# Involution on one core: the running maximum of the logits taken chunk by chunk out of PSUM instead of tap row by tap row out of SBUF

## What is computed

```python
sub2 = x1[:, :, None] - unfold_patches(x2)            # 49 taps, 32 channels
feat = jnp.concatenate([sub2, subp], axis=1)
y = relu(bn_eval(feat, bn1_g, bn1_b, bn1_m, bn1_v))
y = relu(bn_eval(conv1x1(y, cw1), bn2_g, ...))
wgt = softmax(conv1x1(y, cw2, cb2), axis=2)           # over the 49 taps
for i in range(7):
    for j in range(7):
        out = out + patch(x3, i, j) * wgt[:, :, 7 * i + j][:, :, None]
```

## Time and profile before

| | |
|---|---|
| median of 3 runs | 3697.45 us |
| span of the profiled execution, first to last instruction | 3768.7 us |
| step 1 of the third slot, and of the last (15th) | 352.09 and 1635.56 us of the span |
| busy share over the span: PE, DVE, ACT, POOL | 81%, 68%, 53%, 54% |
| mean granted TensorE clock | 0.919 of full speed |

### The profile page before, as it was taken

One profiled execution on the slowest core, in us unless ns is written; L12 is line 12 of the kernel. 1 busy time (PEld: TensorE's weight loads), 2 busy tenths in 40 slices (PEclk: granted clock), 3 DMA queues, 4 the chain that ended last, 5 costly groups with the idle time before them and its releaser, 6 DMA issues. The chain is left out here.

```text
span 3768.7 us, 102003 instructions
## 1 busy us (share of the span) xinstructions
PE 3044.6 (81%) x42638; PEld 1539.3 (41%) x42638; DVE 2563.3 (68%) x2229; ACT 2010.5 (53%) x3451; POOL 2040.6 (54%) x1112
## 2 busy tenths in 40 slices
PE   4767788877777788764999899989999987586797
PEld 1224444433443444432433434343435343364565
DVE  6359999999999999996745755574667456443212
ACT  1175566666555566632676666657566754333120
POOL 1169888889898888874622434060416123332422
PEclk9889999999899999896999999999999998797898
DMA  5621111211111112103111111210221112343344
GB/s 195 194 76 47 58 37 58 61 58 59 52 56 50 57 35 61 51 12 97 27 27 64 41 27 37 74 29 19 61 69 28 27 45 98 115 132 113 123 134 127
DMA packets 169418, 257.31 MB, mean 68 GB/s; under 512 B 81584, under 2 KB 128600, under 8 KB 165912
## 3 DMA queue, kind: packets, MB, share of 16 engines
q1 hardware_dynamic: 157120, 219.82, 19.2%
q0 software_dynamic: 11360, 30.95, 2.6%
q10 hardware_dynamic: 504, 0.05, 0.0%
HBM read 152.23 MB, written 79.27 MB: 61 GB/s over the span
## 5 line engine op out<-in xcount | busy, mean ns | idle before, releaser
L741 PE MATMUL ps<-prod,ident 32*32 32x504 f32 x17472 | 936.4, 646 | 259.4 <-issue 182.7
L678 DVE TENSOR_TENSOR prod<-ps,win 128x3584 f32<-128x3584 f32 x280 | 1054.6, 3789 | 97.6 <-PE ps L741 50.9
L1405 POOL TENSOR_TENSOR pool<-kv 128x768 f32<-128x768 f32 (+1 forms) x200 | 349.8, 1756 | 541.5 <-ACT kv L1539 494.4
L741 PEld LDWEIGHTS ps<-prod,ident 32*32 32x32 f32 x17472 | 382.7, 108 | 464.1 <-issue 412.5
L1583 ACT ACTIVATE phq<-ps 128x896 f32<-128x896 f32 x448 | 391.3, 919 | 80.4 <-PE ps L1915 76.8
L456 POOL TENSOR_TENSOR y<-a1w,x2w 128x1568 f32<-128x1568 f32 x98 | 346.0, 3538 | 132.0 <-PE ps L722 114.9
L465 POOL TENSOR_TENSOR ex<-lg,mx 128x1568 f32<-128x1568 f32 x98 | 345.1, 3541 | 16.1 <-DVE mx L664 15.9
L1915 PE MATMUL ps<-qst,sel 96*128 96x448 bf16 x1120 | 297.2, 362 | 17.0 <-ACT sx L1568 8.4
L560 ACT ACTIVATE ps<-ex 128x448 f32<-128x448 f32 x280 | 148.4, 533 | 296.6 <-DVE prod L678 296.6
L1690 DVE TENSOR_TENSOR pool<-ps,kv 128x1280 f32<-128x1280 f32 (+1 forms) x200 | 295.4, 1480 | 1.1 <-ACT ps L1543 1.1
L482 POOL TENSOR_TENSOR own_a<-ex,win 128x1792 f32<-128x1792 f32 x70 | 262.2, 3746 | 45.9 <-issue 21.6
(11 more groups left out here) (266 smaller groups left out, 5306.3 us busy)
## 6 DMA issues: line engine op xcount, KB each, us to landing
win<-planes SPq DMA_DIRECT2D x14, 2480.0 KB, 9.0
pf<-pf_dram SPq DMA_DIRECT2D x392, 55.1 KB
qst<-qsp SPq DMA_DIRECT2D x96, 196.0 KB, 4.8
planes<-stage SPq DMA_DIRECT2D x7, 1984.0 KB, 7.0
xs<-in_x SPq DMA_DIRECT2D x8, 1568.0 KB, 22.0
conv_dram<-osb SPq DMA_DIRECT2D x56, 224.0 KB, 4.9
t<-in_x SPq DMA_DIRECT2D x28, 448.0 KB, 4.0
xt<-conv_dram SPq DMA_DIRECT2D x28, 448.0 KB, 7.6
```

The source lines that it names most:

```text
L678: v.tensor_tensor(o, w, xw, ALU.mult).then_inc(prod_ready, 1)
L741: mm = pe.matmul(ps[32 * h:32 * h + 32, 4 + r, 0:DENC], diag(ident, r), x[32 * r:32 * r + 32, h].rearrange("p s w -> p (s w)"), start=begi ...
L1405: pool.tensor_tensor(phk[j % 2][0:r, :, ROT_V * DH:FLIN].rearrange("p h (r i) -> p h r i", i=DH), ki.unsqueeze(2).broadcast_to([r, HPG, RO ...
```

## The change

The maximum is now taken from the chunks while they lie in PSUM. `chunkmax(c)` replaces `rowmax`: for chunks 2 to 13, in step c + 3, DVE does two instructions of 128x392, one for each bank, that add the bias and take the maximum with what is there so far. DVE takes bank 1 first while ACT copies bank 0 (`third(c, 0)`), then they change places: ACT's `third(c, 1)` waits for DVE's bank 1, and DVE's bank 0 waits for `third(c, 0)`. The copy of a chunk is thus two instructions, and they come one step later on ACT, with `weights` between them. PE's first(c + 1) waits for both readers. `fold` has four passes instead of three, writes its first pass to banks 0 and 1, and comes in step 16 instead of 17. On PE the order within a step changes from first, pair half 0, second, pair half 1 to pair half 0, first, pair half 1, second. Two more waits are added (PE's first chunk on `maxed`, POOL's last shift on `logit`).

```diff
-MAX_AT = [CH_AT[2 * i + 1] + 3 for i in range(K7)]
+MAX_AT = [t + 2 for t in CH_AT]
 FOLD_AT = MAX_AT[-1]
-EXP_NOW = {FOLD_AT + 1: 0, FOLD_AT + 2: 1}
+EXP_NOW = {18: 0, 19: 1}
...
+                if i == K7 - 1:
+                    pool.wait_ge(logit, 2 * b.g(NCH))
...
-                def third(c):
-                    act.wait_ge(mm2, a.g(c) + 1)
+                def third(c, q):
+                    i, h, k = c // 2, c % 2 * 2 + q, chain_bank(b, c) + q
+                    if q == 0:
+                        act.wait_ge(mm2, a.g(c) + 1)
+                        if b and c % 2 == 0:
+                            act.wait_ge(shifted, b.q(i) + 1)
+                    elif c >= 2:
+                        act.wait_ge(ranmax, NMAX * a.n + 2 * c - 3)
+                    act.activation(lg[:, i, h].rearrange("p j w -> p (j w)"), ps[:, k, 0:CW],
                                    ACT.Identity, bias=par[:, CB2:CB2 + 1]).then_inc(logit, 1)
...
                 for u in range(NPAIR_D if b else 0):
-                    if a and u in CH_AT:
-                        second(CH_AT.index(u))
+                    if a and u - 1 in CH_AT:
+                        third(CH_AT.index(u - 1), 0)
                     if b and u + 2 < NPAIR_D:
                         weights(b, u + 2)
+                    if a and u - 1 in CH_AT:
+                        third(CH_AT.index(u - 1), 1)
                     if b and u + 1 < NPAIR_D:
                         denominators(b, u + 1)
                     if a and u in CH_AT:
-                        third(CH_AT.index(u))
+                        second(CH_AT.index(u))
...
-                    v.tensor_tensor(run[:], lg[:, i], lg[:, 0] if i == 1 else run[:], ALU.max).then_inc(ranmax, 1)
+                    for q in (1, 0):
+                        h, k = c % 2 * 2 + q, chain_bank(b, c) + q
+                        if q == 1:
+                            v.wait_ge(mm2, a.g(c) + 1)
...
+                        else:
+                            v.wait_ge(logit, 2 * a.g(c) + 1)
+                        so_far = (lg[:, 0, h] if c < 4 else run[:, h]).rearrange("p j w -> p (j w)")
+                        v.scalar_tensor_tensor(run[:, h].rearrange("p j w -> p (j w)"), ps[:, k, 0:CW], par[:, CB2:CB2 + 1], so_far,
+                                               ALU.add, ALU.max).then_inc(ranmax, 1)
...
+                    v.wait_ge(logit, 2 * a.g(NCH))
+                    v.tensor_tensor(three, rows[:, :, :, 0:3 * W], rows[:, :, :, 4 * W:], ALU.max).then_inc(ranmax, 1)
...
+                    v.tensor_tensor(left, three[:, :, :, 0:W], rows[:, :, :, 3 * W:4 * W], ALU.max).then_inc(ranmax, 1)
...
+                        if c >= 3:
+                            pe.wait_ge(ranmax, NMAX * a.n + 2 * c - 4)
+                        await_ge(logit, 2 * a.g(c))
...
                 for u in range(NPAIR_D if b else 0):
-                    if a and u in CH_AT:
-                        first(CH_AT.index(u))
                     if b:
                         pair(u, 0)
                     if a and u in CH_AT:
+                        first(CH_AT.index(u))
+                    if b and 2 * u + 1 < ND:
+                        pair(u, 1)
+                    if a and u in CH_AT:
                         second(CH_AT.index(u))
```

More of the change, by code:

```diff
@@ L339 @@
 SCALE_AT = 1
-NMAX = K7 + 1
+NMAX = 2 * (NCH - 2) + 3
 class Blk:
@@ L598, in slot @@
                         if c >= 1:
-                            third(c - 1)
+                            third(c - 1, 0)
+                            third(c - 1, 1)
                         if c % 2 == 0 and c + 2 < NCH:
                             first(c // 2 + 1)
-                    third(NCH - 1)
+                    third(NCH - 1, 0)
+                    third(NCH - 1, 1)
                     expo(a, 0)
@@ L645, in slot, with chunkmax @@
             def slot(a, b):
-                def rowmax(i):
-                    if i == 0:
+                def chunkmax(c):
+                    if c < 2:
                         return
[L649 to L653, removed]
-                    v.tensor_tensor(run[:], lg[:, i], lg[:, 0] if i == 1 else run[:], ALU.max).then_inc(ranmax, 1)
@@ L656, in fold @@
-                def fold():
[L657 to L661, removed]
+                    for q in (1, 0):
+                        h, k = c % 2 * 2 + q, chain_bank(b, c) + q
+                        if q == 1:
+                            v.wait_ge(mm2, a.g(c) + 1)
+                            if c < 4:
+                                v.wait_ge(logit, 2 * a.g(c - 2) + 2)
+                            else:
+                                v.wait_ge(ranmax, NMAX * a.n + 2 * c - 6)
+                            if c == 2 and b and not b.early(1):
+                                v.wait_ge(divided, 2 * b.n)
+                        else:
+                            v.wait_ge(logit, 2 * a.g(c) + 1)
+                        so_far = (lg[:, 0, h] if c < 4 else run[:, h]).rearrange("p j w -> p (j w)")
+                        v.scalar_tensor_tensor(run[:, h].rearrange("p j w -> p (j w)"), ps[:, k, 0:CW], par[:, CB2:CB2 + 1], so_far,
+                                               ALU.add, ALU.max).then_inc(ranmax, 1)
@@ new lines, in fold @@
+                def fold():
+                    three = ps[:, 0:2, 0:RW // 2 * 3 * W].rearrange("p b (h x) -> p b h x", x=3 * W)
+                    rows = run[:].rearrange("p (b h) j w -> p b h (j w)", b=2)
+                    left = rows[:, :, :, 0:W]
+                    v.wait_ge(ranmax, NMAX * a.n + 2 * NCH - 4)
+                    v.wait_ge(logit, 2 * a.g(NCH))
+                    v.tensor_tensor(three, rows[:, :, :, 0:3 * W], rows[:, :, :, 4 * W:], ALU.max).then_inc(ranmax, 1)
+                    v.wait_ge(ranmax, NMAX * a.n + 2 * NCH - 3)
+                    v.tensor_tensor(left, three[:, :, :, 0:W], rows[:, :, :, 3 * W:4 * W], ALU.max).then_inc(ranmax, 1)
+                    v.wait_ge(ranmax, NMAX * a.n + 2 * NCH - 2)
+                    v.tensor_tensor(left, three[:, :, :, W:2 * W], left, ALU.max).then_inc(ranmax, 1)
+                    v.wait_ge(ranmax, NMAX * a.n + 2 * NCH - 1)
@@ L662, in fold @@
                     if b:
                         v.wait_ge(shifted, K7 * a.n)
-                    v.tensor_tensor(mx[:].rearrange("p (h w) -> p h w", w=W), run[:, :, 0], run[:, :, 1], ALU.max).then_inc(maxed, 1)
+                    v.tensor_tensor(mx[:].rearrange("p (b h w) -> p b h w", b=2, w=W), three[:, :, :, 2 * W:], left, ALU.max).then_inc(maxed, 1)
                 def pair(p):
@@ L681, in slot @@
                     if a and u in MAX_AT:
-                        rowmax(MAX_AT.index(u))
+                        chunkmax(MAX_AT.index(u))
                     if a and u == FOLD_AT:
@@ L707, in first @@
                     k = chain_bank(b, c)
+                    if c == 0 and not a.early(1):
+                        pe.wait_ge(maxed, a.n)
                     if b is None:
+                        if c >= 4:
+                            pe.wait_ge(ranmax, NMAX * a.n + 2 * c - 6)
                         if c >= 2:
-                            await_ge(logit, a.g(c) - 1)
+                            await_ge(logit, 2 * a.g(c) - 2)
                     else:
-                        await_ge(logit, a.g(c))
+                        if c >= 3:
+                            pe.wait_ge(ranmax, NMAX * a.n + 2 * c - 4)
+                        await_ge(logit, 2 * a.g(c))
                     y, f = y1[a.qpar(i)], pf[a.qpar(i)]
@@ L773, in slot @@
                     if a and u in CH_AT:
+                        first(CH_AT.index(u))
+                    if b and 2 * u + 1 < ND:
+                        pair(u, 1)
+                    if a and u in CH_AT:
                         second(CH_AT.index(u))
                     if b:
-                        if 2 * u + 1 < ND:
-                            pair(u, 1)
                         for k in range(OWN):
```

## The result

| | median | runs |
|---|---|---|
| before | 3695.51 us | 4, 3691.70 to 3697.88 |
| changed | 3775.33 us | 4, 3774.20 to 3777.57 |

The ratio is 1.0216, with an interval of 1.0203 to 1.0228: the changed kernel is 79.8 us slower. 3760 was forecast, with 3694 to 3785 as its range.

The account below looks back on a forecast made before the run. The slot's end was taken as the bound: own 8's start plus a 13.30 us tail, not DVE's work. +5.2 us a slot times 13 is 68, times 0.98 is 66; with 3697.5 about 3762, said 3760, range 3694 to 3785.

Parts of the forecast that it names:

- tail: Slot's end, from the start of POOL's own 8 to the next pair 0: 13.30 us, whatever DVE does.
- fold ready: Slot's end: after both half copies of the last chunk the fold stands ready 84.2 us after pair 0's start.
- The first chunk: Slot's start: PE's first(0) stands behind half of pair 1, so the chunk chain starts 1.0 us later (0 to 1.3).
- The pace: Chunk chain on ACT: 5.13 us a chunk in eleven early steps, 66.5 us for 13 against 65.55, so +1.0 us.
- its relief buys nothing here: Chunk chain: DVE needs 4.85 us a step, less than the chain, so its saved work brings no time there.
- The clash: Slot's end: own 6 starts 0.5 us ahead of the fold, whose first pass waits for it until 87.4.
- The order: Slot's end: pair 16 and PE's own 6 stand behind the fold, delaying own 8; 3.2 of +5.2 us a slot.
- PE's restart: PE after some 6 us idle: pair 16 with own 6 takes 4.8 us, between 3.5 and 5.9.
- The factor 0.98: Scaling of the sum, the profiled execution being 1.9% longer than the median: 68 us becomes 66.
- the fold did meet POOL: Rival at the slot's end: the fold doesn't meet POOL; 3704 with a fast PE, 3723 with a slow one; chance 0.22.
- the half copies were not at half price: Rival on ACT: half copies cost half a whole one, chain at 4.88; with an unblocked fold 3668; chance 0.13.
- the worst case: Rival on DVE: its small instructions clash with POOL too, 3 us each; two a slot give 3840; chance 0.03.

Follow-up runs that it names:

- e1: Changed kernel with the fold moved back to step 17, behind pair 16: 3757.04 us, 10.5 us faster than the kernel before.
- e2: Changed kernel with PE's first chunk of a slot put ahead of pair 1 again: 3837.86 us, 70.3 us slower than the kernel before on that occasion.
- e3: Changed kernel with PE's adding of own 6 moved from the end of step 16 to its beginning: 3757.17 us, 10.4 us faster than the kernel before.
- e4: Changed kernel with ACT copying the maximum's upper columns to PSUM, so the fold's first pass has one SBUF input: 3815.99 us, 48.5 us slower than before.
- e9: Kernel before, whole row maxima kept, with only its last maximum and the fold moved from step 17 to 16: 3774.04 us, 79.4 us slower than before.
- e8: e1 with ACT's weights issued behind both half copies instead of between them: 3652.70 us, 41.9 us faster than the kernel before.
- e7: e8 plus the edits of e2 and e4: 3640.47 us, 54.1 us faster than the kernel before.

## Why the prediction was right, and where its sizes were off

Start of own 8 and start of the next pair 0, from the slot's start, in the slot shown of each kernel. The difference is the tail, the same within 0.4 us.

| | own 8 | next pair 0 | tail |
|---|---|---|---|
| before | 93.22 | 106.52 | 13.30 |
| changed | 99.46 | 112.54 | 13.08 |
| e1 | 92.93 | 106.06 | 13.13 |
| e2 | 99.15 | 112.24 | 13.09 |
| e3 | 92.44 | 105.58 | 13.14 |
| e4 | 96.76 | 110.22 | 13.46 |
| e9 | 97.75 | 110.82 | 13.07 |
| e8 | 90.75 | 103.88 | 13.13 |
| e7 | 88.81 | 101.93 | 13.12 |

That is the step of the prediction that carried the rest: DVE's busy share of 9 was not the bound, own 8's start was. Its other steps, in us from the slot's start:

| step | forecast | measured |
|---|---|---|
| 1. ReLU 0 | 13.9 | 14.82 |
| 2. pace of the early steps | 5.13 | 5.07 |
| ReLU 13 | 80.4 | 80.72 |
| 3. fold ready | 84.2 | 84.41 |
| own 6 starts on POOL | 83.7 | 83.94 |
| fold ends | 89.6 | 89.7 |
| pair 16 and own 6 on PE | 4.8 | 5.63 |
| own 8 starts | 98.4 | 99.46 |
| tail | 13.3 | 13.08 |
| slot | 111.7 | 112.54 |

- **The first chunk** came 1.9 us later than before, not 1.0. I charged PE half a pair at the rate of a busy PE. At that place its clock is at half, and a pair takes it 4.02 us there (the rows in e2). e2 shows that only half of this reaches the slot's end.
- **The pace** came out right in part by luck. The half copy takes 0.58 us as taken, and the steps 5.07. Over 13 chunks that came to +0.35 us on before instead of +1.0, which made good part of the first error. But the 65.55 us of before are not 13 steps of 5.04, as I read them from their two ends. By the starts of the ReLUs, on the mean of twelve slots, seven of the first eight steps take 4.34 to 4.51 us there, and the one from chunk 10 to chunk 11 takes 10.2. Timeline of DVE and of ACT in the kernel before, between these two:

```profile
1042.25 5.20 DVE L654 TENSOR_TENSOR run<-lg,run 128x1568 f32<-128x1568 f32 x1
```
```profile
1047.92 1.00 ACT L584 ACTIVATE y<-ps,u2c,s2c 128x784 f32<-128x784 f32 x1 [0.60 <-PE ps L722]
1051.28 0.55 ACT L560 ACTIVATE ps<-ex 128x448 f32<-128x448 f32 x1 [2.36 <-DVE prod L678]
```

  The chain ran ahead of DVE and then stood waiting for it, since the row maxima had put DVE behind. The change makes each early step of the chain some 0.7 us longer and takes that stop of 5 us away; the two all but cancel. So "its relief buys nothing here" was wrong, and so was 5.04 as the chain's own pace before; the two errors, some 5 us each, all but cancel. DVE needs 4.89 us a step once nothing holds it, close to my 4.85 (timeline of e8):

```profile
1004.75 3.88 DVE L702 TENSOR_TENSOR prod<-ps,win 128x3584 f32<-128x3584 f32 x1
...
1009.64 3.88 DVE L702 TENSOR_TENSOR prod<-ps,win 128x3584 f32<-128x3584 f32 x1
```

  That is near where the pace stops: e8's 13 chunks come 4.94 us apart on the mean.
- **The clash** and its margin of 0.5 us were right (0.47). e4 prices it at 2.3 us a slot as long as the order is as it is; e3 shows that alone it costs nothing.
- **The order** is the cause: e9, e1 and e3 each show it from another side. In the prediction the whole 3.2 us of the slot's end depended on the fold being ready at 84.2 and pair 16 behind it; that is what happened.
- **PE's restart** was the largest error that reached the slot's end. I took 4.8 us, midway between 3.5 and 5.9; 5.63 is close to the slow end, as PE's clock was at half nearly throughout. Against the 3.5 us at full clock that is 2.1 us of the 5.70 that a slot loses (an estimate from the earlier trace rows and the rows of PE above; no run keeps the clock up with the order as it is). By that own 8 comes 1.06 us later than forecast, and with the shorter tail the slot is 0.84 us longer.
- **The factor 0.98** was a wrong step, though it took off only 1.4 us. The profiled execution of before was 1.9% longer than the median, but all of it in its last stage. Without the factor, the measured 5.70 us times 13 give 74 us; the last divide comes 75.7 us later (1790.1 instead of 1714.4), and the interval of the ratio is 75 to 84 us. The some 4 us between the trace and the median are not placed.

The rivals: the fold did meet POOL (0.22 fell), and the half copies were not at half price (0.13 fell). The maxima didn't clash (614/626/628 ns, min, median and max of 280), so the worst case fell too.

## What to carry to other kernels

Before counting what a busy engine saves, find the release that starts the serial tail of a loop (here a buffer that PE gives back to POOL), and ask of each moved step whether it now stands ahead of that release in some engine's order; one step too early cost here all that the change could give, and one number in the order gave it back. An edit that has this wrong can hide a sound idea: the same chunked maximum is 10 us faster than before when its fold stands a step later, 42 us with ScalarE's weights moved behind the copies as well, and 54 us with the first chunk ahead of pair 1 and the fold kept clear of POOL besides. And if a profiled execution is longer than the median, find the stage that is longer before scaling any sum by it.

## What the runs showed of the hardware

- A clash of DVE with POOL is paid by whoever comes second. With DVE 0.47 us behind, its pass takes 3.97 instead of 0.87 us; with DVE 0.12 us ahead, it takes 0.88 and POOL's multiply 4.31 instead of 3.7.
- PE's granted clock has two levels in these traces. 64 matmul records take 2.31 us at a clock of 1.00 and 4.02 at 0.50. In the changed kernel it stood at 1.00 from 1007 to 1010 us, while PE idled, and at 0.50 from 1011 to 1016 us, in which PE worked for 4.29 us; from 1017 to 1018 it was back at 1.00. A pair costs 1.7 us more by it (4.02 - 2.31). The length of the pause right ahead doesn't tell: e2's pair took 4.02 us behind 4.03 us of idling, but its clock had been at half since before that pause, and e4's took 3.78 behind 4.88. The mean of the stage, 0.91 before and 0.90 now, hides all of this.
- The last stage took 72 us more in one profiled execution, with the wait for its gathered rows at 178.4 instead of 115.3 us. In each profile of e1 to e4 that wait was between 179.3 and 182.1 us, and the kernel before took 3767.5; in the profiles of the last four it was 115.4 to 116.3 us, and before took 3694.6. By its span of 3768.7 us and its wait, the profiled execution of before goes with the first group, while its timed runs (3691.70 to 3697.88) go with the second. What differs between the two was not looked into.
